# Differential attention in a two-layer kernel: GpSimd sums the exponentials over the key tiles and divides; the row maxima come from 32-row tiles spread over two groups

## The chip, the cores and the metric

One core of a Trainium2 chip, float32 throughout. The metric is the device time of one execution of the whole kernel in microseconds (us): the median of the runs of a kernel.

## What is computed

The reference applies two layers to x (4 x 512 x 512). The change touches one stage only, the attention of the second layer ("differential attention"), with 16 heads of two times 16 features:

```python
qkv = x @ W_attn                     # x is layer-normed; q1, k1, q2, k2: (B, T, 16, 16); v: (B, T, 16, 32)
lam = exp(lq1 . lk1) - exp(lq2 . lk2) + LAMBDA_INIT
attn1 = einsum('bthd,bshd->bhts', q1, k1) * scale
attn2 = einsum('bthd,bshd->bhts', q2, k2) * scale
score = softmax(attn1 - lam * attn2, axis=-1)
out = (1.0 - LAMBDA_INIT) * einsum('bhts,bshd->bthd', score, v)
x = x + out.reshape(B, T, E) @ W_proj
```

Nothing is masked. The two products of a head are one product over 32 features, with scale and -lam folded into the queries.

## The kernel before

The kernel runs six stages one after the other; a batch row is a pass, and a stage makes four passes. The stage of the change is `stage_diff_attention` (L1488 ff.). It holds T = 512 queries and keys in TT = 4 tiles of 128, and takes the 16 heads in GROUPS = 4 groups of HG = 4 heads (4 x 32 features = 128 partitions). The work of one group g within a pass:

- `project` (L1603): q and k of a group, four matmuls 128x128x512 each into one bank of PSUM. ScalarE rounds the result to `hi` (`high`, L1741), VectorE subtracts it for the rest `lo` (`low`, L1814), and SP copies hi and lo by DMA (`stack`, L1579), head by head, so that each head's queries `qs` and keys `ks` have 96 rows (hi, lo, hi against hi, hi, lo). A product of these is nearly that of float32, at the speed of one fp32r matmul.
- `rows` (L1620): 16 matmuls a group (head j, query tile tt) give the scores with the queries on partitions, only for the maxima: VectorE takes the maximum of each (`maxima`, L1829). `negate` (L1630) transposes the 128 x 16 maxima, VectorE negates them (`negated`, L1836), and GpSimd stores them by DMA as row 97 of the queries (`store_maxima`, L1907), against a row of ones in the keys.
- `columns` (L1638): the scores again with the keys on partitions, less the maximum by that 97th row: two heads at a time into two banks, key tile st, half (heads 0 and 1, then 2 and 3). ScalarE writes their exponentials to `prob_t` (`exponentials`, L1751), which has two slots for the key tiles.
- `weigh` (L1648): for each key tile four matmuls with v into `acc` (a head to 32 partitions of the output), half 0, and four with a matrix of ones into `acc_sum`, half 1: the sum of the exponentials, accumulated over the four key tiles.
- `finish` (L1844): VectorE takes the reciprocal of `acc_sum` and multiplies `acc` by it into `out_t`. After four groups the output projection (L1706) and the addition to x (L1876) follow.

The order is written out by hand, one `one_pass` for each engine (L1663, L1765, L1852, L1914, L1590). While group g is weighed, the rows of the next group (rg = g+1) and the projections of the one after it (pg = g+2) are worked on; both may belong to the next pass. For key tile st = 0: columns of the second half, 2 rows, project q, columns of tile 1, weigh, columns, 5 rows, weigh with ones; st = 1 the same with 4 rows, k, and 5 rows, and the negation behind it; tiles 2 and 3 have only columns and weigh. The columns (0, 0) of the next group come last. In g = 1 the next pass's normed x is transposed, at the end of g = 3 stand the values v of the next pass and the output projection. VectorE begins a group with `finish` of the group before, and in g = 0 it norms the next pass's x behind the negation.

Rows, projections, the transposed negation, transposes of x, values and output projection share four banks, `banks`, dealt in a fixed order (`Ring`, L67, order in `steps`, L1531). A step may write its bank only when the step four places before has been consumed; every engine waits in its own program order.

Of the kernel before, what the change touches and what calls it, by code (L numbers as in the profile page):

```python
# [32 lines left out]
P = 128  # L33
# [1454 lines left out]
def stage_diff_attention(core, sb, psum, dram, x, consts, scratch):  # L1488
# [15 lines left out]
    lam_v = sb("d_lam_v", [P, 4, D], F32)  # L1504
# [5 lines left out]
    hi = sb("d_hi", [P, 2, T], F32R)  # L1510
# [6 lines left out]
    prob_t = sb("d_prob_t", [P, 2, HG, T], F32)  # L1517
# [8 lines left out]
    ROWS_AT = ((0, 2), (2, 7), (7, 11), (11, 16))  # L1526
    xn_steps = [("xn", k) for k in range(KD)]
    v_steps = [("v", tt) for tt in range(TT)]
    rows_steps = lambda g, a, z: [("row", g, m) for m in range(a, z)]

    def steps(more):  # L1531
# [3 lines left out]
        for g in range(GROUPS):  # L1535
            rg, pg = (g + 1) % GROUPS, (g + 2) % GROUPS
            rows_on, proj_on = more or g + 1 < GROUPS, more or g + 2 < GROUPS
            for half in range(4):
                order += rows_steps(rg, *ROWS_AT[half]) if rows_on else []
                if half in (0, 2) and proj_on:  # L1540
                    order += [("q" if half == 0 else "k", pg)]
            order += [("neg", rg)] if rows_on else []
            order += xn_steps if g == 1 and more else []
# [5 lines left out]
                 + rows_steps(0, 0, ROWS) + [("neg", 0)])  # L1549
# [7 lines left out]
    prob_used = core.sem("d_prob_used")  # L1557
    score_full = core.sems("d_score_full", 2)
    exp_done = core.sems("d_exp_done", 2)
    acc_full = core.sem("d_acc_full")  # L1560
# [3 lines left out]
    FILLS = HG // 2 * TT  # L1564

    with nc.Block() as block:
        @block.sync
        def _(sp):
# [10 lines left out]
            def stack(ring, in_pass, g):  # L1579

                for n, (rows, parts) in enumerate(((qs, (hi, lo, hi)), (ks, (hi, hi, lo)))):
# [18 lines left out]
        def _(pe):  # L1600
            start_at_one(pe, *exp_done, acc_free, *stacked, prob_used, acc_full, *ring.free, *first.free)
# [18 lines left out]
            def rows(ring, in_pass, g, a, z):  # L1620

                for m in range(a, z):
                    j, tt = m // TT, m % TT
                    b, turn = ring.at(("row", g, m), in_pass)
                    pe.wait_ge(ring.free[b], turn)
                    nc.tensor.matmul(banks[b][:], qs[0:3 * E2, g * HG + j, tt * P:(tt + 1) * P],  # L1626
                                     ks[0:3 * E2, g * HG + j, :], start=True, stop=True) \
                        .then_inc(ring.full[b], 1)

            def negate(ring, in_pass, g):  # L1630

                ring.wait_free(pe, in_pass, ("neg", g),
                               consumed=rows_steps(g, ROWS - TT, ROWS))
# [4 lines left out]
            def columns(n, g, st, half):  # L1638

                if st == 0 and half == 0:  # L1640
                    pe.wait_ge(max_in, n * 16 + 16)
# [6 lines left out]
            def weigh(n, g, st, half):  # L1648

                if half == 0:  # L1650
                    if st == 0:
                        pe.wait_ge(acc_free, n + 1)
# [553 lines left out]
```

## Time and profile before

| | us |
|---|---|
| median of 3 runs | 2576.68 (2576.60 to 2576.71) |
| the profiled execution | 2584.38 |
| its span, first to last instruction | 2582.6 |
| TensorE busy (matmul) in the span | 2262.6, 88% |
| VectorE / ScalarE / GpSimd busy | 1771.1 / 920.4 / 1052.6 |
| the stage of the change, first pass to last output | 1940 to 2465 |

Times in the trace are us from the start of the span. PE is TensorE's matmul, PEld its weight load, DVE VectorE, ACT ScalarE, POOL GpSimd, SP the queue of the DMAs. A float32 matmul stands in the trace as two instructions, an fp32r one as one. A granted clock of 1.00 is 2.4 GHz, 0.50 is 1.2 GHz. The profiled execution is 7.7 us (0.3%) longer than the median of the timed ones.

### The profile page before, as it was taken

The page shows a single profiled execution, that of the slowest core. Times are in us where ns is not written, and L with a number is a line of the kernel's source. Part 1 is how long each engine was busy: PE and PEld are TensorE (multiplying, and loading weights), DVE is VectorE, ACT ScalarE, POOL GpSimd, SP SyncE. Part 2 cuts the span into 40 slices and gives each one's busy share as a digit, 9 for nine tenths or more (in the row PEclk, how much of TensorE's full clock was granted, in tenths as well). Part 3 has the DMA queues.
Part 4 walks back from the last instruction along what each step waited for, and adds up shares of the span by engine and source line. Part 5 has one row for each costly group of instructions (what it writes and reads, how often), then busy time and mean ns, then how long its engine had stood idle before and what let it go on. Part 6 is the DMA issues. An engine that isn't in the chain of part 4 may idle for free. (4 is left out here: it accounts for less than half of the span.)

```text
span 2582.6 us, 24445 instructions
## 1 busy us (share of the span) xinstructions
PE 2262.6 (88%) x6992; PEld 1049.2 (41%) x6992; DVE 1771.1 (69%) x2979; ACT 920.4 (36%) x1759; POOL 1052.6 (41%) x789
## 2 busy tenths in 40 slices
PE   6998998999899777774798989989869999999858
PEld 3554444455455443332243434334333333434224
DVE  1887687688768877773688897987745455554454
ACT  1443323334333323331554636446203323232311
POOL 2453333355333424443598888988700000000033
PEclk9999999999999988886899999999979999999878
DMA  6000000000000022225321222221142222121021
GB/s 245 18 21 17 17 25 21 17 17 21 21 17 25 22 88 82 82 82 198 116 91 53 86 83 82 91 77 62 49 131 50 50 49 49 40 58 34 16 98 53
DMA packets 88746, 158.34 MB, mean 61 GB/s; under 512 B 14912, under 2 KB 42432, under 8 KB 86352
## 3 DMA queue, kind: packets, MB, share of 16 engines
q1 hardware_dynamic: 72256, 139.76, 17.1%
q10 hardware_dynamic: 15888, 17.43, 2.1%
q8 instruction: 34, 0.56, 0.1%
q14 instruction: 56, 0.46, 0.1%
q0 software_dynamic: 512, 0.13, 0.0%
HBM read 101.18 MB, written 30.80 MB: 51 GB/s over the span
## 5 line engine op out<-in xcount | busy, mean ns | idle before, releaser
L1389 PE MATMUL c_bank<-c_xn_t,c_weights 128*128 128x512 f32 (+1 forms) x704 | 326.4, 609 | 21.1 <-ACT c_h_t L1429 19.5
L706 POOL TENSOR_SCALAR a_prob<-a_prob,a_rsum 128x256 f32<-128x256 f32 x256 | 147.1, 594 | 466.8 <-DVE a_rsum L634 466.6
L1287 DVE TENSOR_TENSOR_SCAN s_state<-s_decay,s_state 128x512 f32<-128x512 f32 x256 | 305.0, 1210 | 36.1 <-ACT s_decay L1221 36.1
L1237 POOL TENSOR_TENSOR s_state<-s_b_rows,s_delta_u 128x1024 f32<-128x1024 f32 x128 | 301.2, 2363 | 11.2 <-DMA s_b_rows<-scan_bc 8.8
L1221 ACT ACTIVATE s_decay<-s_delta,s_a 128x512 f32<-128x512 f32 x256 | 173.2, 688 | 296.5 <-DVE s_state L1287 269.4
L438 PE MATMUL a_bank<-a_xn_t,a_wq 128*128 128x512 f32 x512 | 227.2, 592 | 0.0
L521 PE MATMUL a_bank<-a_wo,a_out_t 128*128 128x512 f32 x512 | 222.3, 592 | 0.0
L1910 POOL DMA_DIRECT2D d_qs<-d_neg_t x16 | 8.2, 514 | 515.3 <-DVE d_neg_t L1841 515.3
L549 ACT ACTIVATE a_prob<-a_score,a_neg_m 128x256 f32<-128x256 f32 x256 | 117.8, 476 | 278.8 <-DVE a_neg_m L629 278.6
L320 DVE TENSOR_SCALAR f_picks<-f_mask,f_lut_xor,f_lut 128x260 int32<-128x260 int32 x512 | 202.5, 468 | 9.6 <-DVE f_mask L314 1.1
L1762 ACT ACTIVATE d_prob_t<-d_score 128x512 f32<-128x512 f32 x256 | 139.0, 595 | 194.5 <-PE d_score L1645 193.2
L1389 PEld LDWEIGHTS c_bank<-c_xn_t,c_weights 128*128 128x128 f32 (+1 forms) x704 | 128.7, 190 | 179.6 <-issue 176.8
L330 DVE COPY_PREDICATED f_picks<-f_mask,f_picks 128x260 int32<-128x260 int32 x448 | 177.7, 455 | 25.6
L1833 DVE TENSOR_REDUCE d_mx<-d_bank 128x1 f32<-128x512 f32 x256 | 158.6, 683 | 33.4 <-PE d_bank L1626 31.9
L1399 PE MATMUL c_bank<-c_weights,c_h_t 128*128 128x512 f32 (+1 forms) x352 | 168.7, 624 | 0.0
L1250 POOL TENSOR_TENSOR s_group<-s_group,s_state 128x1024 f32<-128x1024 f32 x64 | 151.8, 2372 | 12.5 <-DVE s_state L1295 12.2
L1295 DVE TENSOR_TENSOR s_state<-s_state,s_c 128x1024 f32<-128x1024 f32 x128 | 152.8, 1194 | 0.0
L521 PEld LDWEIGHTS a_bank<-a_wo,a_out_t 128*128 128x128 f32 x512 | 97.3, 190 | 122.5 <-issue 122.5
L438 PEld LDWEIGHTS a_bank<-a_xn_t,a_wq 128*128 128x128 f32 x512 | 97.3, 190 | 109.6 <-issue 108.1
L458 PE MATMUL a_score<-a_k_t,a_q_t 128*128 128x256 f32 (+1 forms) x512 | 132.2, 362 | 0.0
L1608 PE MATMUL d_bank<-d_xn_t,d_w 128*128 128x512 f32 x256 | 120.1, 615 | 4.0 <-ACT d_xn_t L1734 2.7
L1250 POOL TENSOR_TENSOR s_group<-s_state 128x1024 f32<-128x1024 f32 x32 | 75.2, 2350 | 111.0 <-DVE s_state L1295 110.9
(194 smaller groups left out, 3726.6 us busy)
## 6 DMA issues: line engine op xcount, KB each, us to landing
s_b_rows<-scan_bc SPq DMA_DIRECT2D x64, 512.0 KB, 3.6
f_idx<-in_idx SPq DMA_DIRECT2D x64, 130.0 KB, 2.1
ffn_weights<-f_picks SPq DMA_DIRECT2D x64, 130.0 KB, 1.8
r_factor<-in_factors SPq DMA_DIRECT2D x8, 1024.0 KB, 9.0
d_qs<-d_hi SPq DMA_DIRECT2D x128, 64.0 KB, 2.0
d_ks<-d_hi SPq DMA_DIRECT2D x128, 64.0 KB, 2.0
a_wo<-in_wo_t ACTq DMA_DIRECT2D x1, 4096.0 KB, 15.7
scan_y<-m_d_u SPq DMA_DIRECT2D x4, 1024.0 KB, 3.9
```

Of the source, the lines that this page charges most:

```text
L320: last = dve.tensor_scalar(picks[:, j, :], mask[:, 0, :], self.lut_xor[:, j:j + 1], self.lut[:, 2 * j:2 * j + 1], ALU.bitwise_and, ALU.bit ...
L330: last = self.nc.vector.copy_predicated(self.picks[:, j, :], self.mask[:, level + 1, :], self.picks[:, j + half, :])
L438: mm = nc.tensor.matmul(banks[b][:], w[:, k, :], xn_t[:, k, :], start=(k == 0), stop=(k == KD - 1))
L521: mm = nc.tensor.matmul(banks[b][:], out_t[:, tt, r * P:(r + 1) * P], wo[:, g * REPS + r, :], start=(r == 0), stop=(r == REPS - 1))
L1221: self.nc.scalar.activation(self.decay[u % 2][:], self.delta[:, h % 2, e, :], ACT.Exp, scale=self.a[:, h % 2 * 2 + e, n:n + 1]).then_inc(s ...
L1237: pool.tensor_tensor(self.state[:, s], row.broadcast_to([P, 2, T]), self.delta_u[:, h % 2], ALU.mult) \
L1250: pool.tensor_tensor(group, old if n == 1 else group, self.state[:, c % self.SLOTS], ALU.add) \
L1287: dve.tensor_tensor_scan(self.state[:, s, e, :], self.decay[u % 2][:], self.state[:, s, e, :], 0.0, ALU.mult, ALU.add).then_inc(self.scann ...
L1295: dve.tensor_tensor(self.state[:, s], self.state[:, s], row.broadcast_to([P, 2, T]), ALU.mult) \
L1389: mm = nc.tensor.matmul(banks[b][0:width[o], :], weights[:, lo:lo + width[o]], xn_t[:, k, :], start=(k == 0), stop=(k == KD - 1))
L1399: mm = nc.tensor.matmul(banks[b][:], h_t[0:width[o], o, tt * P:(tt + 1) * P], weights[0:width[o], W_DOWN + o * D:W_DOWN + (o + 1) * D], st ...
L1833: nc.vector.tensor_reduce(mx[:, g, m // TT, m % TT:m % TT + 1], banks[b][:], AX_X, ALU.max) \
```

## The change

- The matmuls with ones (`weigh`, half 1) go. GpSimd adds the exponentials of key tiles 1, 2 and 3 onto those of tile 0 in `prob_t` (three additions of 128 x 2048 a group). `total` then sums over the 128 keys with four matmuls with ones, once a group, in key tile 0 of the next group (for g = 3 between the values). `prob_t` gets a third slot (`slot`); the space comes from `lam_v`, which is now part of it.
- `finish` is split: ScalarE takes `acc` out of PSUM, scaled (`take`); VectorE takes the reciprocal (`invert`), now behind the low part of k; GpSimd multiplies (`divide`).
- `rows` reads `hi` itself, head j on its 32 partitions, in place of the 96 stacked rows: hi times hi only, 32-row tiles of the array, one matmul for each of four heads and a query tile (a "part"). `hi` is kept for two groups.
- The 16 maxima of a group are spread over two groups: parts 0 and 1 in key tiles 2 and 3 two groups ahead, parts 2 and 3 in key tiles 0 and 1 one group ahead, each a run of four. The negation comes behind key tile 2's columns. Before the first pass parts 0 and 1 of group 1 are added.
- TensorE waits for the stacked copies ahead of the columns of their group. In g = 0 VectorE's norm is split around maxima part 1.

The diff, cut to its core:

```diff
-    hi = sb("d_hi", [P, 2, T], F32R)
+    hi = sb("d_hi", [P, 2, 2, T], F32R)
-    prob_t = sb("d_prob_t", [P, 2, HG, T], F32)
+    prob_t = sb("d_prob_t", [P, 3, HG, T], F32)
+    lam_v = prob_t[:, 0]
...
-            for half in range(4):
-                order += rows_steps(rg, *ROWS_AT[half]) if rows_on else []
-                if half in (0, 2) and proj_on:
-                    order += [("q" if half == 0 else "k", pg)]
+            for part, kind in ((2, "q"), (3, "k")):
+                order += row_part(rg, part) if rows_on else []
+                order += [(kind, pg)] if proj_on else []
+            order += row_part(pg, 0) if proj_on else []
             order += [("neg", rg)] if rows_on else []
+            order += row_part(pg, 1) if proj_on else []
...
+    def slot(g, st):
+        return 1 if st % 2 else (g + st // 2) % 2 * 2
...
-            def rows(ring, in_pass, g, a, z):
+            def rows(ring, in_pass, g, tt):
+                for _, _, m in row_part(g, tt):
+                    j = m % HG
+                    head = slice(j * E2, (j + 1) * E2)
                     b, turn = ring.at(("row", g, m), in_pass)
                     pe.wait_ge(ring.free[b], turn)
-                    nc.tensor.matmul(banks[b][:], qs[0:3 * E2, g * HG + j, tt * P:(tt + 1) * P],
-                                     ks[0:3 * E2, g * HG + j, :], start=True, stop=True) \
+                    nc.tensor.matmul(banks[b][:], hi[head, g % 2, 0, tt * P:(tt + 1) * P], hi[head, g % 2, 1, :],
+                                     start=True, stop=True).then_inc(ring.full[b], 1)
...
+            def total(n, g):
+                pe.wait_ge(added, (n + 2) * (TT - 1))
+                pe.wait_ge(rsum_done, n + 1)
+                for j in range(HG):
+                    mm = nc.tensor.matmul(acc_sum[j * VD:(j + 1) * VD, :], consts.ones[:, 0:VD],
+                                          prob_t[:, slot(g, 0), j, :], start=True, stop=True)
+                mm.then_inc(summed, 1)
...
                         if st < 2 and rows_on:
-                            rows(ring, i, rg, *ROWS_AT[2 * st])
+                            rows(ring, i, rg, 2 + st)
                         if st < 2 and proj_on:
                             project(ring, i, "qk"[st], pg)
+                        if st >= 2 and proj_on:
+                            if st == 2:
+                                pe.wait_ge(hi_done, (n + 3) * 2)
+                            rows(ring, i, pg, st - 2)
                         if st == 0:
                             columns(n, g, 1, 0)
-                        weigh(n, g, st, 0)
+                        weigh(n, g, st)
                         if st < TT - 1:
                             columns(n, g, st + 1, 1)
-                        if st < 2 and rows_on:
-                            rows(ring, i, rg, *ROWS_AT[2 * st + 1])
-                        weigh(n, g, st, 1)
-                        if st == 1 and rows_on:
+                        if st == 0 and g:
+                            total(n - 1, g - 1)
+                        if st == 2 and rows_on:
                             negate(ring, i, rg)
...
+            def exponentials(n, g, st, half):
+                if half == 0 and st != 2:
+                    act.wait_ge(added, n * (TT - 1) + (2, 3, 0, 4)[st])
+                    act.wait_ge(weighed, n * TT + (3, 4, 0, 6)[st])
+                elif half == 0:
+                    act.wait_ge(summed, n + 1)
...
+            def take(n, g):
+                act.wait_ge(weighed, (n + 2) * TT)
+                nc.scalar.activation(out_t[:, g, :], acc[:], ACT.Copy, scale=1.0 - LAMBDA_INIT).then_inc(acc_free, 1)
...
+            def invert(n):
+                dve.wait_ge(summed, n + 2)
+                dve.wait_ge(out_ready, n + 1)
                 nc.vector.reciprocal(rsum[:], acc_sum[:]).then_inc(rsum_done, 1)
...
+                    for st in range(2):
+                        if rows_on:
+                            maxima(ring, i, rg, 2 + st)
+                        if proj_on:
+                            low(ring, i, n + 2, "qk"[st], pg)
                     if g:
-                        finish(n - 1, g - 1)
+                        invert(n - 1)
+                    if proj_on:
+                        maxima(ring, i, pg, 0)
                     if rows_on:
                         negated(ring, i, n + 1, rg)
...
+            def add(n, g, st):
+                for s in range(2):
+                    pool.wait_ge(exp_done[s], n * FILLS + st * 2 + 2 + 1)
+                if st == 1:
+                    pool.wait_ge(weighed, (n + 1) * TT + 1)
+                else:
+                    pool.wait_ge(added, (n + 1) * (TT - 1) + st - 1)
+                base = prob_t[:, slot(g, 0)]
+                nc.gpsimd.tensor_tensor(base, base, prob_t[:, slot(g, st)], ALU.add).then_inc(added, 1)
+            def divide(n, g):
+                pool.wait_ge(rsum_done, n + 2)
+                pool.wait_ge(acc_free, n + 2)
+                nc.gpsimd.tensor_tensor(out_t[:, g, :], out_t[:, g, :], rsum[:], ALU.mult).then_inc(out_ready, 1)
             def one_pass(i, more):
                 for g in range(GROUPS):
+                    n = i * GROUPS + g
+                    add(n, g, 1)
+                    if g:
+                        divide(n - 1, g - 1)
+                    add(n, g, 2)
                     if more or g + 1 < GROUPS:
                         store_maxima(ring, i, (g + 1) % GROUPS)
                     if g == 0 and more:
                         norm_gpsimd(nc, pool, norm, consts.minus_half, i + 1)
+                    add(n, g, 3)
+                divide(i * GROUPS + GROUPS - 1, GROUPS - 1)
```

## Rows read from the trace of the kernel before

**Rows 1.** Windows, the passes: busy PE, PEld, DVE, ACT, POOL; clock; DMA share, GB/s.
```profile
1940.00:2465.00 525.00, 489.43 (x2030) 200.44 (x2029) 269.97 (x382) 161.94 (x296) 10.59 (x18) 0.98 0.18 43
```

**Rows 2.** Timeline, TensorE, one group (start, length, what, idle before): g=2, first pass.
```profile
1997.90 0.99 PE L1645 MATMUL d_score<-d_qs,d_ks 97*128 97x512 f32 x2 [0.71 <-ACT d_prob_t L1762]
...
1998.72 0.62 PE L1626 MATMUL d_bank<-d_ks,d_qs 96*128 96x512 f32 x2
...
1999.19 3.60 PE L1608 MATMUL d_bank<-d_xn_t,d_w 128*128 128x512 f32 x8
...
2003.18 1.06 PE L1659 MATMUL d_acc<-d_prob_t,d_v 128*32 128x512 f32 x8
...
2004.17 0.86 PE L1645 MATMUL d_score<-d_qs,d_ks 97*128 97x512 f32 x2
...
2004.87 1.69 PE L1626 MATMUL d_bank<-d_ks,d_qs 96*128 96x512 f32 x5
...
2009.24 3.70 PE L1608 MATMUL d_bank<-d_xn_t,d_w 128*128 128x512 f32 x8
```

**Rows 3.** Timeline, TensorE: starts of groups in first, second, last pass; output projection.
```profile
1940.58 1.28 PE L1645 MATMUL d_score<-d_qs,d_ks 97*128 97x512 f32 x2 [0.32 <-ACT d_prob_t L1762]
...
1969.28 0.99 PE L1645 MATMUL d_score<-d_qs,d_ks 97*128 97x512 f32 x2 [0.45 <-ACT d_prob_t L1762]
...
2023.48 0.73 PE L1645 MATMUL d_score<-d_qs,d_ks 97*128 97x512 f32 x2
...
2024.67 0.99 PE L1645 MATMUL d_score<-d_qs,d_ks 97*128 97x512 f32 x2 [0.45 <-ACT d_prob_t L1762]
...
2077.88 1.04 PE L1645 MATMUL d_score<-d_qs,d_ks 97*128 97x512 f32 x2
...
2104.70 0.99 PE L1645 MATMUL d_score<-d_qs,d_ks 97*128 97x512 f32 x2 [0.45 <-ACT d_prob_t L1762]
...
2375.65 0.89 PE L1645 MATMUL d_score<-d_qs,d_ks 97*128 97x512 f32 x2 [0.60 <-ACT d_prob_t L1762]
...
2402.73 0.90 PE L1645 MATMUL d_score<-d_qs,d_ks 97*128 97x512 f32 x2 [0.60 <-ACT d_prob_t L1762]
...
2424.58 0.99 PE L1645 MATMUL d_score<-d_qs,d_ks 97*128 97x512 f32 x2 [0.51 <-ACT d_prob_t L1762]
...
2445.66 15.70 PE L1706 MATMUL d_bank<-d_wp,d_out_t 128*128 128x512 f32 x32 [4.20 <-DVE d_out_t L1849]
```

**Rows 4.** Timeline, ScalarE and VectorE: same group; last row: norm applied in g=0.
```profile
2002.82 0.69 ACT L1748 ACTIVATE d_hi<-d_bank,d_coef 128x512 fp32r<-128x512 f32 x1 [3.30 <-PE d_bank L1608]
...
2005.31 5.66 DVE L1833 TENSOR_REDUCE d_mx<-d_bank 128x1 f32<-128x512 f32 x9 [0.90 <-PE d_bank L1626]
...
2013.60 0.69 DVE L1825 TENSOR_TENSOR d_lo<-d_bank,d_hi 128x512 fp32r<-128x512 f32 x1 [2.63 <-ACT d_hi L1748]
...
1967.66 1.92 DVE L190 TENSOR_SCALAR d_xn<-x_res,d_mean_var,d_rstd 128x512 f32 x4 [1.16 <-POOL d_rstd L204]
```

**Rows 5.** By source line: durations ns min/median/max; last row: landing of L1910's DMA.
```profile
L1043 POOL TENSOR_TENSOR r_factor_sum<-r_factor_sum,r_factor x8: 4547/4790/5039, 954.4 to 1148.2; 128x2048 f32<-128x2048 f32 x8
...
L2050 POOL TENSOR_TENSOR g_gy<-g_y,g_z x16: 1255/1272/1445, 2473.0 to 2542.0; 128x512 f32<-128x512 f32 x16
...
L1847 DVE RECIPROCAL d_rsum<-d_acc_sum x16: 3347/3358/3359, 1969.5 to 2441.5; 128x512 f32<-128x512 f32 x16
...
DMA to landing us min/median/max: 1.7/1.9/2.0
```

**Rows 6.** Busy time and granted clock (PEclk) in single microseconds.
```profile
1931.00:1932.00 1.00, 0.90 (x2) 0.31 (x2) 1.00 (x3) 0.00 (x0) 0.00 (x0) 0.72 0.31 74
...
2404.00:2405.00 1.00, 0.87 (x3) 0.26 (x2) 0.96 (x2) 0.84 (x3) 0.00 (x0) 1.00 0.00 0
2405.00:2406.00 1.00, 0.34 (x4) 0.16 (x8) 1.00 (x2) 0.57 (x2) 0.00 (x0) 0.94 0.06 16
2406.00:2407.00 1.00, 1.00 (x8) 0.00 (x0) 0.81 (x2) 0.00 (x0) 0.00 (x0) 0.50 0.00 0
```

More of the change, by code:

```diff
@@ L1525, in stage_diff_attention @@
     ROWS = HG * TT
-    ROWS_AT = ((0, 2), (2, 7), (7, 11), (11, 16))
     xn_steps = [("xn", k) for k in range(KD)]
     v_steps = [("v", tt) for tt in range(TT)]
-    rows_steps = lambda g, a, z: [("row", g, m) for m in range(a, z)]
+    row_part = lambda g, part: [("row", g, m) for m in range(part * HG, (part + 1) * HG)]
+    all_rows = lambda g: [step for part in range(TT) for step in row_part(g, part)]
     def steps(more):
@@ L1579, in stack @@
             def stack(ring, in_pass, g):
-                for n, (rows, parts) in enumerate(((qs, (hi, lo, hi)), (ks, (hi, hi, lo)))):
+                high = hi[:, g % 2]
+                for n, (rows, parts) in enumerate(((qs, (high, lo, high)), (ks, (high, high, lo)))):
                     b, turn = ring.at(("qk"[n], g), in_pass)
@@ L1640, in columns @@
                 if st == 0 and half == 0:
+                    for m in range(2):
+                        pe.wait_ge(stacked[m], (n + 1) * COPIES + 1)
                     pe.wait_ge(max_in, n * 16 + 16)
@@ L1856, in one_pass @@
                     rows_on, proj_on = more or g + 1 < GROUPS, more or g + 2 < GROUPS
-                    if g:
-                        finish(n - 1, g - 1)
-                    for half in range(4):
-                        if rows_on:
-                            maxima(ring, i, rg, *ROWS_AT[half])
-                        if half in (0, 2) and proj_on:
-                            low(ring, i, n + 2, "q" if half == 0 else "k", pg)
+                    for st in range(2):
[3 more added lines that the diff above has]
+                            low(ring, i, n + 2, "qk"[st], pg)
+                    if g:
+                        invert(n - 1)
+                    if proj_on:
+                        maxima(ring, i, pg, 0)
                     if rows_on:
@@ L1866, in one_pass @@
                     if g == 0 and more:
-                        norm_vector(nc, dve, norm, x, i + 1)
+                        norm_stats(nc, dve, norm, x, i + 1)
+                    if proj_on:
+                        maxima(ring, i, pg, 1)
+                    if g == 0 and more:
+                        norm_apply(nc, dve, norm, x, i + 1)
                     if g == 1 and more:
                         features(ring, i)
-                finish(i * GROUPS + GROUPS - 1, GROUPS - 1)
                 if more:
-                    values(ring, i)
+                    values(ring, i, 0)
+                invert(i * GROUPS + GROUPS - 1)
+                if more:
+                    values(ring, i, 2)
                 for tt in range(TT):
@@ L1899, in _ @@
                     low(first, 0, g, kind, g)
-            values(first, 0)
-            maxima(first, 0, 0, 0, ROWS)
+            for tt in (0, 2):
+                values(first, 0, tt)
+            for tt in range(TT):
+                maxima(first, 0, 0, tt)
             negated(first, 0, 0, 0)
+            for tt in range(2):
+                maxima(first, 0, 1, tt)
             passes(dve, one_pass)
```

105 lines of the change are left out of this document (45 added, 60 removed).

## The prediction

> **What bounds the kernel now.** I read first the busy time of the engines over the stage that the change touches: TensorE works 489 of 525 us, VectorE 270, ScalarE 162, GpSimd 11 [rows 1]. So TensorE sets the pace here, and GpSimd is free. Then TensorE's own sequence through one group of four heads [rows 2]: it starts (call this moment a) with the second half of key tile 0 and comes back to the same place 26.77 us later [rows 2, 3]. Its gaps are short (0.71 us at the start). Everything else hangs on it: ScalarE and VectorE wait for the two projections [rows 4]. Last, the places where each group starts [rows 3]: 26.8 us for g=0 (2077.88 to 2104.70), 28.62 for g=1, 26.77 for g=2, 53.21 for g=3 with the values and the output projection; in the last pass 27.08 (g=1), 21.85 (g=2), and 21.08 from g=3's start to the output projection.
>
> **What it takes off TensorE.** Four sets of ones-matmuls per group become one. A set takes 0.99 us from its start to the next work (2003.18 to 2004.17) [rows 2]: three go, 3.0 us a group. Sixteen row matmuls follow each other at best at 0.235 us (1998.72 to 1999.19 for two [rows 2]), 3.8 us in all. On 32-row tiles a set of four costs between one matmul (0.235) and four (0.94). No row shows a row tile; the nearest are the weighing matmuls, four column tiles at once: x8 in 1.06 us, where x8 of the projection, one after another, take 3.60 [rows 2]. I take the row tiles as running together too: 2.8 us a group. On TensorE alone, 5.8 of 26.8 us go.
>
> The Trainium skill ("TensorE: Matmul & The Clock Gate", Measured speedup vs the span model) gives 3.07 times for four row tiles of K=32; by it a set would cost an estimated 0.31 us instead of 0.235. No run here shows it yet.
>
> **What it puts in.** (1) Three GpSimd adds of 128x2048 a group. The same form stands in the trace: 4.55 to 5.04 us, median 4.79 [rows 5]; I take 4.8. (2) A GpSimd division, 128x512: 1.27 us. (3) ScalarE takes the sum out of PSUM, about as its 0.69 us on the same shape [rows 4]; hidden, it has 363 us spare. VectorE's 0.69 us multiplication goes, its 3.36 us reciprocal [rows 5] stays but moves behind low(k). (4) Rows come in fours on four banks, so each projection waits for the first maximum of its four; before, two rows stood ahead of q.
>
> Busy, GpSimd needs 3 x 4.8 + 1.3 + 0.5 = 16.2 us a group: it isn't full. What counts is the order on its queue: add 1, divide (the group before), add 2, the maxima's DMA, add 3. The DMA lets TensorE start the next group's first scores, so divide and add 2 come onto the path.
>
> **One group g=2, by hand, from a = 0,** each engine in program order, about 0.1 us from one engine's end to another's start:
> - rows (rg, 2) start at 0.8 [rows 2], reach VectorE 0.44 later (2004.87 to 2005.31 [rows 2, 4]), first maximum 1.26 to 1.86 (0.6 each: 5.66 us for 9 [rows 4]); q starts at 1.95, where it now starts at 1.3.
> - high(q) at 5.6 (3.63 after q's start [rows 2, 4]); weigh(0) 5.9; columns(1,1) 6.9 (1.35 after high); total 7.65; columns(2,0) 8.65; rows (rg, 3) 9.2; first maximum to 10.25; k at 10.35.
> - low(k) at 14.7 (4.36 after k's start [rows 2, 4]), to 15.3. Only then the reciprocal, to 18.7; divide 18.8 to 20.05; add 2 to 24.85; DMA issued 25.0, landed after 1.9 (row 97 of the queries [rows 5]); columns(0,0) 26.95; the next a is 1.2 later (2023.48 to 2024.67 on TensorE [rows 3]): **28.15**.
> - Meanwhile the negation waits for a bank behind the reciprocal (19.3), rows (pg, 1) go to 21.5, weigh(3) to 22.8. TensorE is then idle for 4.1 us. Add 1 (7.7 to 12.5) and add 3 (ends 3.4 after the next columns(0,0), before exp(1,0)) hold nobody.
>
> So g=2 goes from 26.77 to 28.15: +1.4. The saving on TensorE turns into a wait for GpSimd.
>
> **The other groups** in the same way. g=0 has no reciprocal, division and total in it: k starts at 10.1, exp(2,1) ends 16.3, add 2 to 21.2, columns at 23.3, next a 24.5: -2.3. Its norm moves: the applying (1.92 us [rows 4]) now stands behind maxima (pg, 1) and so ahead of g=1's first maximum, and q starts 1.65 later: g=1 29.8, +1.2. g=3: weigh(3) ends 22.8 and values go on without waiting for the DMA; total waits for add 3 at 30.3, hidden behind two of the four values: next a 52.0, -1.2. Per pass -0.9, three passes: -2.7.
>
> Last pass: g=0 -2.3; g=1 28.15 against 27.08, +1.1; g=2 has no projections, but add 1 starts at 5, divide ends 13.5, add 2 18.3, next a 21.6: -0.3. g=3: add 1 5.6 to 10.4, divide, add 2, add 3 in a row to 21.2, total, reciprocal 3.36, divide: output projection at 27.3 against 21.08: +6.2. Start: two parts of group 1's rows are ahead of the first pass, 8 x 0.6 = 4.8 us of VectorE, all but 0.7 beside the maxima's DMA. Last pass and start +5.4; sum without the clock **+2.7 us**.
>
> **The clock.** The granted clock is 0.98 of full speed over the stage [rows 1]. It began to fall (0.72 in that microsecond) where TensorE had been kept to one row matmul per maximum, and fell to 0.50 (1.2 GHz) after 0.87 and 0.34 us busy in two microseconds [rows 6]. Both are milder than what I expect here: from 19.8 to 26.95 only some 2 us of matmul work. The price of one such stretch is in the trace: group 0 of pass 0 starts at the low clock and takes 28.70, that of pass 1 26.82 [rows 3], so 1.9. It lies on the path, since q does. Ten projections q follow such an idle stretch (g=1, 2, 3 of three passes, g=1 of the last): 10 x 1.9 = 19, and 1 for the weighing of the last two groups. **+20 us.** Bounds: 0 (clock holds) and 7 a start (both projections, 3.6 us each [rows 2], at half speed; against it stands that the group that started low paid only 1.9).
>
> The Trainium skill (same page, What's actually happening) says the throttled state is the default and activity releases it. By that rule the idle ends of the groups cost the clock each time; the two falls in rows 6 agree.
>
> **Sum:** +2.7 + 20 = +23 us. The profiled execution took 2584.4 us (span 2582.6) and would take 2607; the median shown is 7.7 below it, so I put the same 23 us on 2576.7: **2599 us**.
>
> **Rivals.**
> - *The clock holds* (or falls only now and then): chain as above, +3, 2579. For it: gaps of a microsecond in these groups leave the clock at 1.00. Against: 4 us idle, after a thin stretch. Chance 0.12.
> - *TensorE stays the bound, faster.* If the next scores needn't wait for divide and add 2, each group gives 5.8 us less 2 x 1.0 for the waits on the first maximum, 3.8 x 16 = 61 us, less 6 at the very end: 55, 2522. It decides at one point: whether the maxima's DMA lands before weigh(3) ends (22.8). From low(k)'s end at 15.3, reciprocal and DMA leave 2.2 us for divide and add 2 together, where the rows say 6.1. Anything that puts the DMA ahead of add 2 would do it; the text of the program doesn't. Chance 0.14, mostly for an error in my order of events; part of it is a smaller gain (2550 to 2570).
> - *The clock stays low longer,* through k as well, or GpSimd's adds run at 5.04 and above (its 128x512 products run between 1.26 and 1.45 [rows 5]): another 1.5 to 3 us a group start, 2615 to 2635. Chance 0.16.
> - *GpSimd's price is smaller than the row:* the Trainium skill ("GPSIMD Engine Reference", 3.1) has 4.50 us for this add and advises VectorE for elementwise work; by its figure 11 chains lose 0.3 each, 3 us less. The trace differs upward (4.79), and the measurement decides; the time stays with the forecast.
> - *The row tiles don't run together:* the sets then cost 0.85, but VectorE at 0.6 a maximum and the DMA set the pace. Nothing changes in sum.
>
> **Chances and range.** Forecast 0.58 (2588 to 2612); clock holds 0.12; faster rival 0.14; slower still 0.16. What a measurement can tell from no change is about 0.2%, 5 us. The clock-holds case (2572 to 2585) puts 0.08 within it, 0.02 below; half slips of the chain give a few more: faster 0.18, same 0.10, slower 0.72. The range leaves out the faster rival's core (2522) and the top of the slow one: 2560 to 2625.
>
> **What would show it.** In the changed profile: GpSimd adds of 4.8 us; TensorE idle some 4 us at the end of g=1 and g=2, released by the DMA of the maxima, itself issued right behind add 2; the division right after the reciprocal; group distances near 24.5, 32, 30 and 54; the granted clock at 0.5 at the head of g=1 to 3. I am wrong if the DMA goes out before TensorE reaches weigh(3)'s end, if the distances are near 23, or if the clock stays at 1.00.

## The result and the profile after

The changed kernel takes **2627.95 us** (median of 4 runs, 2626.88 to 2628.84), the kernel before beside it 2576.69 us (4 runs): a ratio of **1.0198, 95% interval 1.018 to 1.0216**. Forecast were 2599 us and 2560 to 2625 us: slower is right, the size is not, +51 us in place of +23. The profiled execution took 2628.84 us with a span of 2627.0, 44.4 more than the span before; the other 7 us are the profiled execution of before, which took 2584.4. Run again beside the experiments it gave 2576.3 to 2587.8 us, with medians of 2578.9 to 2581.5; its second trace (e0) has the same distances between groups. Against those medians the change costs 46 to 49 us, and its own executions lie close together.

The same stretch of passes in windows (columns as in [rows 1]):

```profile
1940.00:2465.00 525.00, 445.91 (x1559) 171.30 (x1559) 251.74 (x356) 165.92 (x301) 231.46 (x77) 0.87 0.18 42
```

TensorE was busy 489 of 525 us and is now busy 446, GpSimd went from 11 to 231, and the granted clock fell from 0.98 to 0.87. TensorE no longer sets the pace. The costliest groups of GpSimd in the stage (count, busy and mean ns, idle time before with its releaser):

```profile
L1957 POOL TENSOR_TENSOR d_prob_t<-d_prob_t 128x2048 f32<-128x2048 f32 x48 | 217.2, 4526 | 216.1 <-ACT d_prob_t L1781 215.7 <-POOL d_prob_t L1957 0.2
L1963 POOL TENSOR_TENSOR d_out_t<-d_out_t,d_rsum 128x512 f32<-128x512 f32 x16 | 20.4, 1273 | 81.9 <-DVE d_rsum L1872 81.9
```

The timeline of one group g=2 of the first pass, all engines, from k to the next group's first scores (start, length, what, idle before). It answers to [rows 2, 4]:

```profile
2018.63 0.51 PE L1637 MATMUL d_bank<-d_hi 32*128 32x512 f32 x4
2019.92 3.70 PE L1618 MATMUL d_bank<-d_xn_t,d_w 128*128 128x512 f32 x8 [0.78 <-DVE d_mx L1857]
...
2024.28 0.69 DVE L1849 TENSOR_TENSOR d_lo<-d_bank,d_hi 128x512 fp32r<-128x512 f32 x1 [2.63 <-ACT d_hi L1770]
...
2024.89 3.35 DVE L1872 RECIPROCAL d_rsum<-d_acc_sum 128x512 f32<-128x512 f32 x1
...
2026.64 0.51 PE L1637 MATMUL d_bank<-d_hi 32*128 32x512 f32 x4
2027.08 1.06 PE L1668 MATMUL d_acc<-d_prob_t,d_v 128*32 128x512 f32 x8
...
2028.32 1.27 POOL L1963 TENSOR_TENSOR d_out_t<-d_out_t,d_rsum 128x512 f32<-128x512 f32 x1 [5.74 <-DVE d_rsum L1872]
...
2029.55 4.51 POOL L1957 TENSOR_TENSOR d_prob_t<-d_prob_t 128x2048 f32<-128x2048 f32 x1
...
2034.00 0.55 POOL L1944 DMA_DIRECT2D d_qs<-d_neg_t  x1
2034.57 4.53 POOL L1957 TENSOR_TENSOR d_prob_t<-d_prob_t 128x2048 f32<-128x2048 f32 x1
2035.84 1.22 PE L1657 MATMUL d_score<-d_qs,d_ks 97*128 97x512 f32 x2 [3.54 <-DMA d_qs<-d_neg_t]
```

This is the forecast path link by link: low(k), reciprocal, division, add 2, the maxima's DMA, and TensorE idle for 3.54 us until it lands. The windows of this place (columns as above) show what the idle time does to the clock:

```profile
2032.00:2033.00 1.00, 0.31 (x4) 0.00 (x0) 1.00 (x2) 0.60 (x1) 1.00 (x1) 1.00 0.43 96
2033.00:2034.00 1.00, 0.00 (x0) 0.00 (x0) 0.15 (x1) 0.00 (x0) 1.00 (x1) 0.89 0.29 68
2034.00:2035.00 1.00, 0.00 (x0) 0.00 (x0) 0.00 (x0) 0.00 (x0) 0.98 (x3) 0.50 0.01 2
2043.00:2044.00 1.00, 1.00 (x3) 0.48 (x2) 0.00 (x0) 0.00 (x0) 0.00 (x0) 0.50 0.00 0
2044.00:2045.00 1.00, 1.00 (x3) 0.40 (x3) 0.00 (x0) 0.00 (x0) 0.00 (x0) 0.99 0.00 0
```

The clock is at 0.50 (1.2 GHz) in every microsecond from 2034 to 2044, which takes in the next q (2040.11, 5.63 us). So far the forecast. What it did not have stands in the second pass, between g=0 and g=1 (timeline of GpSimd, VectorE and TensorE, ordered by start):

```profile
2113.70 0.55 POOL L1944 DMA_DIRECT2D d_qs<-d_neg_t  x1
2115.88 1.03 POOL L204 TENSOR_TENSOR d_rstd<-d_var_eps,minus_half 128x4 f32<-128x4 f32 x1 [1.64 <-DVE d_var_eps L182]
2116.90 4.51 POOL L1957 TENSOR_TENSOR d_prob_t<-d_prob_t 128x2048 f32<-128x2048 f32 x1
2117.24 1.28 PE L1657 MATMUL d_score<-d_qs,d_ks 97*128 97x512 f32 x2 [0.26 <-ACT d_prob_t L1781]
2118.09 4.97 DVE L190 TENSOR_SCALAR d_xn<-x_res,d_mean_var,d_rstd 128x512 f32 x4
...
2122.99 2.47 DVE L1857 TENSOR_REDUCE d_mx<-d_bank 128x1 f32<-128x512 f32 x4
2123.72 6.49 PE L1618 MATMUL d_bank<-d_xn_t,d_w 128*128 128x512 f32 x8 [4.47 <-DVE d_mx L1857]
```

The four operations that apply the norm take 4.97 us, before 1.92 [rows 4], and they run beside add 3 of GpSimd. They stand ahead of the first maximum of the group, so TensorE waits 4.47 us for q, and q then runs at the low clock, 6.49 us in place of 3.60. The first operation alone (timeline of VectorE), and the clock while q runs:

```profile
2118.09 3.61 DVE L190 TENSOR_SCALAR d_xn<-x_res,d_mean_var,d_rstd 128x512 f32 x1
```

```profile
2124.00:2129.00 5.00, 5.00 (x6) 1.89 (x7) 1.46 (x3) 0.00 (x0) 0.00 (x0) 0.50 0.00 0
```

Add 3 ends at 2121.41, and the first operation ends at 2121.70, 0.3 us behind it; the other three are through 1.4 us later. The third pass shows the same 0.3 (2264.85, 2265.15). So one operation lasts until the add is over; the four are not each slower.

By distances of groups, taken as in [rows 3]: 29.1, 34.8, 31.2 and 54.7 us in the first pass, 25.2, 35.2, 28.4 and 54.6 in the second and third, 25.4, 32.1, 23.7 and 28.4 in the last.

### The profile page after: what moved, and what is told of

The parts are those of the page before. It is cut to its first block and busy times, and to the rows that moved or that the text cites. A ratio compares the mean times of both kernels' runs of the same rounds, so it can differ in the third digit from the quotient of the medians.

```text
span 2627.0 us, 24002 instructions
## 1 busy us (share of the span) xinstructions
PE 2249.1 (86%) x6608; PEld 1031.6 (39%) x6608; DVE 1765.6 (67%) x2963; ACT 931.2 (35%) x1775; POOL 1289.9 (49%) x853
## 5 line engine op out<-in xcount | busy, mean ns | idle before, releaser
L1389 PE MATMUL c_bank<-c_xn_t,c_weights 128*128 128x512 f32 (+1 forms) x704 | 325.8, 608 | 21.4 <-ACT c_h_t L1429 19.8
L1957 POOL TENSOR_TENSOR d_prob_t<-d_prob_t 128x2048 f32<-128x2048 f32 x48 | 217.2, 4526 | 216.1 <-ACT d_prob_t L1781 215.7
L1618 PE MATMUL d_bank<-d_xn_t,d_w 128*128 128x512 f32 x256 | 142.1, 709 | 34.0 <-DVE d_mx L1857 31.2
L1657 PE MATMUL d_score<-d_qs,d_ks 97*128 97x512 f32 x256 | 120.0, 538 | 41.5 <-DMA d_qs<-d_neg_t 26.2
```

What stands on the lines that cost most here:

```text
L1389: mm = nc.tensor.matmul(banks[b][0:width[o], :], weights[:, lo:lo + width[o]], xn_t[:, k, :], start=(k == 0), stop=(k == KD - 1))
L1957: nc.gpsimd.tensor_tensor(base, base, prob_t[:, slot(g, st)], ALU.add).then_inc(added, 1)
```

## The experiments

**e0: the kernel before, once more,** unchanged.

> The kernel before, unchanged, profiled once more. The timed runs of it lie at 2576.6 to 2577.5 us, its profiled execution at 2584.4, while the changed kernel's profiled execution (2628.8) lies only 0.9 above its median. If those 7.7 us belong to one execution (a part of a stage at the low clock), this one comes out near 2577 and the difference stands in one stage. If profiling costs it, it comes out at 2584 again.

2583.53 us, group distances as in [rows 3], within 0.04 us. By the expectation this is the outcome "if profiling costs it", but that isn't shown either: in e1 and e2 below the profiled execution has the shortest time of its four. The 49 executions of this kernel beside the experiments lie anywhere from 2576.3 to 2587.8 us. Where the 7 us lie stays open; not in the distances between the groups, which the two traces share, so these can be compared group by group.

**e1: the norm away from GpSimd's add.** Add 3 of g=0 starts only when the norm has been applied.

```diff
                     if g == 0 and more:
                         norm_gpsimd(nc, pool, norm, consts.minus_half, i + 1)
+                        pool.wait_ge(norm.xn_ready, (i + 2) * TT)
                     add(n, g, 3)
```

> Only GpSimd's third add in g=0 waits until VectorE has applied the norm. Theory A (VectorE's four normalizing instructions, from SBUF to SBUF, are held up while a GpSimd add runs: 4.97 us for four in the changed kernel, 1.92 before): they take 1.92 again, q of g=1 starts 3 us sooner, three passes give 8 to 10 us: 2619. Rival B (they are slow for another reason, and the long distance of g=1, 35.2 us, comes from the low clock alone): 4.97 stays, 2628, or more since the add is later.

2617.4 us (2609.69 to 2620.31), ratio 1.0152 [1.0135, 1.0168]: 10.5 us less than the changed kernel. The trace stands at 2609.69 us, 7 to 11 below the other three executions, so only distances inside the stage are read from it. The source line of the norm, first the changed kernel, then e1 (count, min/median/max ns, first and last start):

```profile
L190 DVE TENSOR_SCALAR d_xn<-x_res,d_mean_var,d_rstd x16: 533/538/3606, 1886.8 to 2266.0; 128x512 f32 x12, 128x512 f32<-128x512 f32 x4
```

```profile
L190 DVE TENSOR_SCALAR d_xn<-x_res,d_mean_var,d_rstd x16: 539/542/546, 1874.4 to 2243.9; 128x512 f32 x12, 128x512 f32<-128x512 f32 x4
...
2102.42 1.91 DVE L190 TENSOR_SCALAR d_xn<-x_res,d_mean_var,d_rstd 128x512 f32 x4
...
2104.63 4.50 POOL L1957 TENSOR_TENSOR d_prob_t<-d_prob_t 128x2048 f32<-128x2048 f32 x1 [3.39 <-DVE d_xn L190]
...
2104.98 6.30 PE L1618 MATMUL d_bank<-d_xn_t,d_w 128*128 128x512 f32 x8 [1.39 <-DVE d_mx L1857]
```

The same four operations without the add beside them take 1.91 us, and q waits 1.39 instead of 4.47 us. In one of the changed kernel's four, 3606 ns stand for 540. The overlap is the cause, not the operation's new place. The passes (from one negation of g=1's maxima, which stands in g=0, to the next) last 142.5, 140.1 and 143.1 us, in the changed kernel 145.9, 143.5 and 143.4: 3.4 and 3.3 less, so the later add costs nothing there, but in the third only 0.3. There q of g=2 fell to the low clock (5.40 us, before that 3.70) and took most of it back.

**e2: the clock held up.** Matmuls that nobody needs (into the bank of the sums, while it is free) fill TensorE's idle ends.

```diff
+            def keep_busy(n, count):
+                pe.wait_ge(rsum_done, n)
+                for _ in range(count):
+                    nc.tensor.matmul(acc_sum[:], consts.ident[:], v[:, 0, :], start=True, stop=True)
...
                             rows(ring, i, rg, 2 + st)
+                            if st == 0 and g:
+                                keep_busy(n, 5 if g == 1 and more else 1)
...
                     if g + 1 < GROUPS:
+                        keep_busy(n + 1, (2, 1, 4)[g])
                         columns(n + 1, g + 1, 0, 0)
```

> Matmuls that nobody needs fill TensorE's waits at the group ends and ahead of q, into the bank of the sums. Theory A (the path runs through GpSimd, and q at half speed adds 2 to 2.9 us at 8 of the 10 group heads that follow an idle stretch): the granted clock stays at 1.00, q takes 3.6 instead of 5.6 to 6.5, the time falls by 15 to 20 us to 2610. Rival B (TensorE's own work is the bound): the added matmuls, about 13 us a pass, lengthen it to 2650 or more. Rival C (the clock follows something else): q stays at 5.6 or more.

2607.9 us (2606.68 to 2609.72), ratio 1.0113 [1.0096, 1.013]: 20.0 us less than the changed kernel, although TensorE does more. The timeline at the same place:

```profile
2112.95 4.56 PE L1684 MATMUL d_acc_sum<-d_v,ident 128*128 128x512 f32 x10
2118.02 3.70 PE L1618 MATMUL d_bank<-d_xn_t,d_w 128*128 128x512 f32 x8 [0.51 <-DVE d_mx L1865]
```

q takes 3.70 us, though it comes as late as before against the norm, which is still held. So the clock is a cost of its own: at least 20 us, since the added matmuls can cost something themselves. In sum that is what the forecast booked.

**e3: divide last.** The division moves behind add 3, off the way of the maxima.

```diff
                     add(n, g, 1)
-                    if g:
-                        divide(n - 1, g - 1)
                     add(n, g, 2)
...
                     add(n, g, 3)
+                    if g:
+                        divide(n - 1, g - 1)
```

> GpSimd divides after its third add, not between the first and the second; nothing else moves. Theory A (path: k, low part of k, reciprocal, divide, second add, DMA of the maxima, next columns): the second add starts some 16 to 17 us after the group's start instead of 21 to 23, the DMA is then bound by the negation behind the reciprocal (21.5); g=1 and g=2 each lose 3 to 4 us, also in the last pass: 7 x 3.3 = 23, 2603 to 2607. Rival B (GpSimd has too much work in all): the same work in another order, 2628.

2607.17 us (2604.9 to 2614.08), ratio 1.0105 [1.0088, 1.0122]. The median is as expected. The trace stands at 2614.08 us, 6 to 9 above the other three executions, with a mean granted clock of 0.914 against their 0.917; it can't tell where those gained the rest. In it the path did get shorter: 7.06 us from low(k) to the DMA, in the changed kernel 9.72 (2024.28 to 2034.00).

```profile
2195.01 0.69 DVE L1849 TENSOR_TENSOR d_lo<-d_bank,d_hi 128x512 fp32r<-128x512 f32 x1 [2.63 <-ACT d_hi L1770]
...
2197.11 4.54 POOL L1957 TENSOR_TENSOR d_prob_t<-d_prob_t 128x2048 f32<-128x2048 f32 x1 [3.81 <-ACT d_prob_t L1781]
...
2201.99 1.94 PE L1668 MATMUL d_acc<-d_prob_t,d_v 128*32 128x512 f32 x8
2202.07 0.55 POOL L1944 DMA_DIRECT2D d_qs<-d_neg_t  x1 [0.42 <-issue]
...
2203.85 7.83 PE L1626 MATMUL d_bank<-d_w,d_xn_t 128*128 128x512 f32 x16
```

But its passes last 143.1, 143.3 and 143.1 us against 145.9, 143.5 and 143.4, so the second and third hardly got shorter. In the second pass g=1 gains 2.0 us and g=2 0.8, and g=3 loses 2.7 (57.3 against 54.6). Those 2.7 are low clock: q of g=3 takes 6.62 us in place of 5.52, the weighing at 2201.99 1.94 in place of 1.06, the values behind it 7.83 in place of 7.13. The last pass is 7.6 us shorter from its negation in g=0 to the output projection. Whether the path shows in the passes once the clock is held, e8 and e10 put to the test.

**e8: e1, e2 and e3 together,** their three edits in one kernel.

> The changed kernel with three edits at once: the norm kept off GpSimd's add 3, dummy matmuls that hold the clock, and add 3 and the division behind the store (divide last). Theory: the 2.7 us that divide last took off the path per group were eaten by the clock in the passes, so with the clock held they show: two groups of a pass have their head on that path, so a pass is 139.6 (clock held) - 3 (norm) - 5.4 = about 131, and the run about 2600 - 20 = 2580 us (2574 to 2590). Rival: the shorter path brings nothing in the passes because something else ends there (the values or the rows of TensorE's own queue), then the pass stays at 136 to 137 and the run at about 2597 us.

2594.35 us (2588.36 to 2597.42), ratio 1.0058 [1.0039, 1.0078]; passes 135.9, 136.0 and 140.8 (why the third is longer stays open). The time is above the expected 2574 to 2590 and near the rival's 2597. The timeline shows why it decides nothing:

```profile
2157.10 0.55 POOL L1952 DMA_DIRECT2D d_qs<-d_neg_t  x1 [0.41 <-issue]
...
2157.98 3.70 PE L1684 MATMUL d_acc_sum<-d_v,ident 128*128 128x512 f32 x8
2161.12 1.02 PE L1657 MATMUL d_score<-d_qs,d_ks 97*128 97x512 f32 x2
```

The scores follow the dummies without a gap. With the DMA out at 2157.10, what held TensorE to 2161 was my own filling, sized for the longer path of e2. So a shorter path could not show here.

**e10: the same with fewer dummies.**

```diff
-                                keep_busy(n, 5 if g == 1 and more else 1)
+                                keep_busy(n, 3 if g == 1 and more else 1)
...
-                        keep_busy(n + 1, (2, 1, 4)[g])
+                        if g != 1:
+                            keep_busy(n + 1, 2 if g == 0 else 1)
```

> e8 with fewer dummy matmuls. In e8's trace the next first scores followed a row of four dummies without idle time (2157.98, columns at 2161.12) though the maxima's DMA had been issued at 2157.10, so would have landed at about 2159.1; five dummies also held q of g=1 to 2109.86 where its first maximum could have been there at about 2108.7. So the fillers themselves held TensorE. Here one instead of four at the end of g=2, none at the end of g=1, three instead of five before q of g=1. Theory: the path that ends in the maxima's DMA shows once the fillers are short: -2.0, -0.4 and -1.2 a pass, passes of 132 to 133 instead of 136.0, and the run 3 x 3.6 = 11 below e8, about 2583 us (2576 to 2588). Rival: the shorter path brings nothing, another wait (the exponentials, the maxima) takes the place of the fillers, or the clock falls again: passes of 135 or more, the run at 2592 us or more.

2585.94 us (2583.24 to 2591.41, 10 runs), ratio 1.0023 [1.0012, 1.0034]; the second and third pass 133.0 and 132.9, below the 135.4 of the kernel before. The scores that open g=2 and g=3 in the second pass (the view ends at 2162):

```profile
2136.13 0.99 PE L1657 MATMUL d_score<-d_qs,d_ks 97*128 97x512 f32 x2 [0.71 <-ACT d_prob_t L1790]
...
2161.78 0.50 PE L1657 MATMUL d_score<-d_qs,d_ks 97*128 97x512 f32 x1 [0.45 <-ACT d_prob_t L1790]
```

g=2 takes 25.65 us, in the changed kernel 28.4 with the clock up there too: 2.8 less, about the 2.7 by which divide last shortens the path. So the path does set that group. The 2.7 are less than the 3 to 4 us a group that I had expected in e3.

**e4: the maxima before add 2.** The negation comes right behind k, VectorE does it ahead of the reciprocal, GpSimd sends behind add 1 and divides last.

```diff
                     add(n, g, 1)
-                    if g:
-                        divide(n - 1, g - 1)
-                    add(n, g, 2)
                     if more or g + 1 < GROUPS:
                         store_maxima(ring, i, (g + 1) % GROUPS)
+                    add(n, g, 2)
...
+                    if rows_on:
+                        negated(ring, i, n + 1, rg)
                     if g:
                         invert(n - 1)
```

> The maxima are finished first: the negation comes right behind k on TensorE and right behind the low part of k on VectorE, ahead of the reciprocal, and GpSimd sends them off between its first and second add; it divides last. Theory A: the DMA lands some 18 us after the group's start, before TensorE has done its weighing (22.8), and TensorE or its bank waits set the distance again: about 24 for g=0 and g=2, 29 for g=1, 53 for g=3, and the clock stays up. Per pass 14 us less than the changed kernel, in the last pass 8 less: 2578, level with before. If the order of the maxima is not the cause: 2600 or more.

2594.22 us (2593.86 to 2597.0, 6 runs), ratio 1.0044 [1.003, 1.0059]; passes of 140.0 us. A miss by 16 us. With the DMA early, TensorE reaches g=1 sooner (g=0 takes 18.3 us, in the changed kernel 25.2), and there the norm (4.93 us for four) and the clock stand as before: q waits 4.67 us and takes 6.05.

**e5: e4 and e1 together.**

> As the run before with the maxima first, and in g=0 GpSimd's third add waits for VectorE's norm. Theory A: the four normalizing instructions take 1.92 instead of 4.97, q of g=1 starts 3 us sooner in three passes: 9 us less than without, 2569, which would be below the kernel before (2577). Rival: the add, now later, holds up the exponentials of g=1 and gives it back: no difference.

2585.1 us (2583.09 to 2586.35, 10 runs), ratio 1.0014 [1.0003, 1.0025]; passes 136.6. The step from e4 is the 9 us expected; the level isn't, again by 16 us (2569 expected). The low clock is still there, q takes 5.2 to 5.9 us in g=1, 2 and 3 of each pass. That it makes up the 16 us was not measured.

**e6: each projection ahead of its rows.** TensorE does q and k first and the four row tiles behind the next scores, so VectorE's maxima run while it works. ScalarE sends the maxima, the norm is applied first in its group, the reciprocal and the division come last.

```diff
-                        if st < 2 and rows_on:
-                            rows(ring, i, rg, 2 + st)
                         if st < 2 and proj_on:
                             project(ring, i, "qk"[st], pg)
...
                             columns(n, g, st + 1, 1)
+                        if st < 2 and rows_on:
+                            rows(ring, i, rg, 2 + st)
...
                         exponentials(n, g, st + 1, 1)
+                    if more or g + 1 < GROUPS:
+                        store_maxima(ring, i, (g + 1) % GROUPS)
                     take(n, g)
```

> All waits found so far taken off the path: each projection stands ahead of its four rows instead of behind them, the maxima are negated right behind parts 2 and 3 and sent off by ScalarE's queue, the reciprocal comes last on VectorE, the division last on GpSimd, the norm's statistics open g=0 and its application opens g=1 (GpSimd's third add may still hold it, but VectorE is idle there). By the durations of the traces a group takes about 21 us (TensorE bound, clock up), g=1 25, g=3 48: a pass 115 where the kernel before has 135.4 and the changed one 143.4. Theory A (the sums on GpSimd and the row tiles do save TensorE 5 us a group, and only the order lost it): 2505 to 2530, below both kernels. Rival (GpSimd's 16 us a group, or its hold on VectorE, costs by itself): not below 2575.

**2530.25 us** (2525.06 to 2534.11), ratio **0.9801 [0.978, 0.9821]**: 98 us below the changed kernel and 49 below the kernel before. TensorE's timeline in a group g=1:

```profile
2085.58 0.99 PE L1658 MATMUL d_score<-d_qs,d_ks 97*128 97x512 f32 x2 [0.45 <-ACT d_prob_t L1782]
2086.41 3.60 PE L1619 MATMUL d_bank<-d_xn_t,d_w 128*128 128x512 f32 x8
2089.44 1.03 PE L1658 MATMUL d_score<-d_qs,d_ks 97*128 97x512 f32 x2
...
2092.19 0.51 PE L1638 MATMUL d_bank<-d_hi 32*128 32x512 f32 x4
...
2094.20 3.60 PE L1619 MATMUL d_bank<-d_xn_t,d_w 128*128 128x512 f32 x8
```

Here neither q nor k waits for a maximum, and both run at 3.60 us. Groups in the passes take 21.2 to 25.8 us, those with the values 51.1 to 51.4. Passes: 119.3, 118.9 and 120.1. The clock isn't up everywhere: q of g=3, and in the third pass of g=1, still takes 4.8 to 5.3 us.

**e7: e6, but GpSimd sends the maxima behind add 2,** as the changed kernel does.

```diff
+                    add(n, g, 1)
+                    add(n, g, 2)
+                    if more or g + 1 < GROUPS:
+                        store_maxima(ring, i, (g + 1) % GROUPS)
+                    add(n, g, 3)
```

> The same, but GpSimd sends the maxima off behind its second add, as in the changed kernel. That add ends about 19.3 us after the group's start, some 2 us behind the negation: theory A expects the next columns 1.5 to 2 us later in each group that waits for them (g=0 and g=2, 8 times): 10 to 16 us more than with ScalarE's queue. If the DMA's place on GpSimd's queue does not matter, both take the same.

2544.84 us (2543.53 to 2548.13), ratio 0.9866 [0.985, 0.9883]: sending from GpSimd behind add 2 costs 14.6 us, even with everything else in good order. Issue to landing of this DMA, first e6, then e7:

```profile
DMA to landing us min/median/max: 1.8/1.8/3.9
```

```profile
DMA to landing us min/median/max: 1.7/2.0/2.1
```

So the transfer itself is 0.2 us slower at most. The place in the queue is the larger part: in a group g=1 of e7 the maxima were negated at 2109.75 and the DMA went out at 2111.68, when add 2 had ended; in e6 it goes out 0.1 us after the negation.

**e9: e6 with the sums on TensorE.** No adds on GpSimd; four sets of ones-matmuls a group, as before.

```diff
+                    for j in range(HG):
+                        mm = nc.tensor.matmul(acc_sum[j * VD:(j + 1) * VD, :], consts.ones[:, 0:VD],
+                                              prob_t[:, slot(g, st), j, :], start=(st == 0), stop=(st == TT - 1))
...
-                    for st in range(1, TT):
-                        add(n, g, st)
```

> The order of e6 (projection ahead of its rows) with the sums made by matmuls with ones over all four key tiles, as in the kernel before, and no adds on GpSimd. Theory: TensorE is the bound in that order, so three more sets of matmuls with ones in each of 16 groups, about 3 us a group at the high clock, show in full: 2530 + 45 = about 2575 us (2560 to 2585). Rival: in that order there was room on TensorE and the adds bring nothing, the row tiles and the order gave all: 2530 us, within 8.

2542.81 us (2542.16 to 2544.76), ratio 0.9857 [0.9839, 0.9876]. Between the two theories and within neither, nearer the rival: the adds on GpSimd are worth 12.6 us, not 45, though three sets a group still cost TensorE 0.9 to 1 us each. The edit moves one thing more, the reciprocal from the end of VectorE's group to its start, and what that does alone was not run. The windows of both over their passes, first e6:

```profile
1940.00:2388.00 448.00, 427.69 (x1608) 164.76 (x1607) 252.45 (x357) 171.72 (x312) 239.33 (x66) 0.95 0.21 50
```

```profile
1940.00:2400.00 460.00, 443.15 (x1990) 172.08 (x1989) 250.68 (x355) 171.14 (x312) 22.61 (x18) 0.99 0.21 49
```

e6 leaves TensorE 20 us idle and has a clock of 0.95; e9 has 17 and 0.99. Which wait ends last in e6 was not taken apart. The larger gain, 36 us of the 49, came with the row tiles and the order, without any add on GpSimd; the two were not run apart.

## Why the prediction was wrong in size

The span grew by 44.4 us. Cut at the starts of g=1, with the forecast beside it: up to the first g=1 +2.1 (forecast -1.6); three passes +26.6 (forecast +14.4, of it 17.1 for the clock); from the last g=1 to the output projection +14.1 (forecast +9.9); the output projection, 17.03 us against 15.70 in [rows 3], +1.3 (forecast 0). That is 21.4 us more than forecast: 9.2 for the norm in the passes and 3.0 for the rest of them, 4.2 in the last pass, 3.7 at the start, 1.3 at the end. Another 7 come from the base: the forecast took off again the 7.7 us by which the profiled execution of before stood above its median, while the changed kernel's executions all lie at 2626.9 to 2628.8, the profiled one at their top.

- **The path: right at g=2.** Reciprocal 3.35, division 1.27, add 2, DMA, landing, TensorE idle 3.54 us (forecast 4.1). g=2 with the high clock takes 28.4 us, forecast 28.15, and with the division off the path 25.65 (e10). At the end of g=1 the 4 us of idle time did not come: 1.71 us in the first pass and none later, since the transposes of x fill it. The add was booked at 4.8 us and took 4.53. The Trainium skill ("GPSIMD Engine Reference", 3.1) has 4.50 us for it, and this case's 48 adds agree; the slower rows 5 stood in another stage.
- **The norm: the step that failed.** "the applying (1.92 us [rows 4]) now stands behind maxima (pg, 1) and so ahead of g=1's first maximum": the order is right, the price is not. I took it from a stretch in which GpSimd was idle, and the change fills GpSimd just there. It is 4.97 us, +3.05 in each of three passes, 9.2 of the 12.2 us missing there, and e1 gave back 10.5 in all. (By groups, with the booked clock in it: g=0 took 0.7 to 0.9 a pass more than forecast, g=1 3.1 to 3.5, g=3 0.7, and g=2 1.1 more in the first pass and 1.6 less in the others.) The trace of before had a warning, the same operation in another stage, in which GpSimd works about 380 of 490 us (what each of its instructions ran beside was not taken apart):

```profile
L190 DVE TENSOR_SCALAR c_xn<-x_res,c_mean_var,c_rstd x16: 532/1968/2562, 1202.7 to 1681.8; 128x512 f32<-128x512 f32 x16
```

I had priced the new work on GpSimd only as time on its own queue, not for what it does to VectorE. The Trainium skill ("GPSIMD Engine Reference", 8) says that the two share their SBUF interfaces and contend where VectorE is in a 2-port mode or has two SBUF inputs; e1 shows the contention for this form, which of the two it is no run here shows.
- **The clock: right in sum, wrong by places.** Booked at 1.9 us a head. Compared with e2, g=1 lost 2.6 (35.2 against 32.65) and g=3 2.4, since q takes 5.5 to 6.5 us and the scores and rows ahead of it are slow too; but q at g=2 took 3.70 in the second and third pass, in which TensorE had no idle time behind the transposes of x, and 5.86 in the first, in which it had 1.71 us. Booked 20, measured 20.0: that the two are equal is luck. The passes gave e2 14.1 where 17.1 were booked, the last pass 4.0 where 2.9 were.
- **Group 0 of the first pass: booked wrongly.** I gave it -2.3. Before and after it starts at the low clock, and took 28.70 and 29.12: in the changed kernel the clock falls again at k, which waits for its first maximum. Its k, first before, then after:

```profile
1953.84 3.70 PE L1608 MATMUL d_bank<-d_xn_t,d_w 128*128 128x512 f32 x8
```

```profile
1955.14 5.40 PE L1618 MATMUL d_bank<-d_xn_t,d_w 128*128 128x512 f32 x8 [0.77 <-DVE d_mx L1857]
```

In other passes g=0 took 25.2, forecast 24.5.
- **The last pass: too short by 4.2.** g=1 took 32.1 (forecast 30.05 with the clock), g=2 23.7 (about 22). e2 has 28.4 for g=1, so the clock took 3.6 there, not 1.9, and 0.3 are left over the 28.15. The rest, 1.7 at g=2 and 0.5 at g=3, stays open.
- **The row tiles: together, but at twice the price.** Four in 0.51 us, the weighing behind them 0.44 after their start (2026.64, 2027.08). The forecast allowed 0.235 to 0.94 and took 0.235; the 0.31 that it named beside it is too low as well. So the row matmuls save an estimated 3.8 - 4 x 0.44 = 2.0 us a group, not 2.8. It cost nothing in the sum, since TensorE's work was not the bound. The wait of 0.77 us for the first maximum is there at q and k.
- **The rivals.** "TensorE stays the bound, faster" did not come. It was reachable: e6, which takes the division and the adds off the maxima's way and the maxima off TensorE's, gave 49 us where that rival had 55. That the two are near each other bears out neither of its terms: the three sets of ones-matmuls, booked at 48 us in all, were worth 12.6 (e9), and the 2.0 us a group taken off for the waits at q and k are gone in e6. "The clock stays low longer" (through k as well; 2615 to 2635) holds the measured time, but k was slow in the first group only; more than half of the miss is the norm and the base.

## What to carry to other kernels

Before work goes to an engine that is free, look up what runs beside it: price each operation of the neighbour on the same memory both with and without it, from rows of both kinds. An idle engine's queue is not free either. A DMA that another engine waits for belongs on a queue with nothing long ahead of it (14.6 us here), and waits that leave TensorE with little work cost their length and the clock of what follows (20 us here).

## What the runs showed of the hardware

- The norm's VectorE operation from SBUF to SBUF, 128x512, takes 540 ns alone and up to 3606 ns if it starts while GpSimd adds 128x2048: it ends 0.3 us after the add (2121.41, 2121.70). Four together take 4.97 in place of 1.91 us. VectorE's 256 maxima, which read PSUM, keep their time beside the adds: 681 ns in the median and 693 at most in both kernels.
- Four matmuls on tiles of 32 rows run together: 0.51 us for the four, 0.44 to the start of the next; one of 96 rows took 0.235 to the next.
- Matmuls whose result nobody uses brought 20 us by the clock alone, and were themselves a cost once they lasted longer than the wait that they filled (3 us in the second pass, from e8 to e10).
- Executions of one kernel on one core scatter by up to 11 us (2576.4 to 2587.8), so one profiled execution is good for distances inside it, not for a median. Nor are its distances those of every execution: e3's trace has a mean granted clock of 0.914, its three other executions 0.917.
